# A five-layer graph network on one core: the first layer reads a transposed copy, the first and the fifth use a split ring

## The reference

```python
def _sage_conv(x, src, dst, Wl, bl, Wr):
    msg_sum = segment_sum(x[src], dst, num_segments=N_NODES)
    deg = segment_sum(ones_like(src), dst, num_segments=N_NODES)
    mean = msg_sum / maximum(deg, 1.0)[:, None]
    return mean @ Wl.T + bl + x @ Wr.T

x = layernorm(x + conv_a2(relu(conv_a1(x))))
x = layernorm(x + conv_b3(relu(conv_b2(relu(conv_b1(x))))))
```

## Time and profile before

| | us |
|---|---|
| median of 3 runs | 5494.6 (5491.9 to 5495.12) |
| the profiled execution | 5473.94 |
| its span, first to last instruction | 5472.3 |
| PE busy | 5178.4 |
| DVE busy | 3574.3 |
| ACT busy | 2560.0 |
| POOL busy | 2278.1 |
| groups of a1 and the end of its pass, window | 159.5 to 922 |
| groups of a2, window | 948 to 1821 |
| b1 and b2 | 1821 to about 4258 |
| groups of b3, window | 4292 to 5462 |

### The profile page before, as it was taken

How to read it: one execution, slowest core, us unless ns; L and a number is a source line. 1 busy time by engine, 2 the same in 40 slices (tenths; PEclk the granted TensorE clock), 3 DMA queues, 4 the chain that set the end, 5 groups by cost and what they waited for, 6 DMA issues and landing times. The chain is left out here.

```text
span 5472.3 us, 161658 instructions
## 1 busy us (share of the span) xinstructions
PE 5178.4 (95%) x44358; PEld 5110.7 (93%) x44359; DVE 3574.3 (65%) x9610; ACT 2560.0 (47%) x7254; POOL 2278.1 (42%) x2959
## 2 busy tenths in 40 slices
PE   1999998999999899999989999999999899999999
PEld 0899998889888899999989999999999899999999
DVE  4344444777777788888866666666666455555555
ACT  0343433777777433333333333333333466666666
POOL 1665655555555344444432322322222333333332
PEclk9999999999999999999999999999999999999999
DMA  1555554666667566666655555555555566666666
GB/s 29 150 168 164 172 167 143 202 202 206 205 200 208 164 194 192 194 195 195 193 165 177 173 178 176 174 179 174 174 180 169 178 217 219 217 219 220 216 219 195
DMA packets 1322822, 1006.82 MB, mean 184 GB/s; under 512 B 70406, under 2 KB 1278627, under 8 KB 1322756
## 3 DMA queue, kind: packets, MB, share of 16 engines
q1 hardware_dynamic: 1247044, 825.23, 48.6%
q0 software_dynamic: 75712, 180.76, 10.7%
HBM read 645.58 MB, written 360.13 MB: 184 GB/s over the span
## 5 line engine op out<-in xcount | busy, mean ns | idle before, releaser
L1043 PE MATMUL f_product_b<-f_ring_b,f_onehot_b 128*128 x6272 | 996.5, 281 | 0.0
L690 PE MATMUL m_product_a<-m_ring_a,m_onehot_a 128*128 x6272 | 959.8, 276 | 0.0
L1043 PEld LDWEIGHTS f_product_b<-f_ring_b,f_onehot_b 128*128 128x128 f32 x6272 | 855.8, 188 | 0.0
L1099 ACT ACTIVATE f_ring_b<-f_e_product_b,t_rec_all 128x256 f32 (+1 forms) x784 | 328.9, 471 | 1099.1 <-PE f_e_product_b L1056 1091.1
L792 DVE TENSOR_TENSOR m_onehot_a<-iota_all,t_win_all 128x512 f32<-128x512 f32 x784 | 537.5, 686 | 454.4 <-PE m_product_a L690 388.4
L690 PEld LDWEIGHTS m_product_a<-m_ring_a,m_onehot_a 128*128 128x128 f32 x6272 | 829.5, 193 | 0.0
L1037 PE MATMUL f_product_b<-b_r_all,f_t_hi_b 128*128 128x256 f32 x2352 | 723.2, 307 | 0.0
L1039 PE MATMUL f_product_b<-b_r_all,f_t_lo_b 128*128 128x256 f32 x2352 | 661.0, 281 | 0.0
L1038 PE MATMUL f_product_b<-b_r_all,f_t_hi_b 128*128 128x256 f32 x2352 | 659.4, 280 | 0.0
L686 PE MATMUL m_product_a<-a_r_all,m_t_full_a 128*128 128x128 f32 x3136 | 608.0, 276 | 0.0
L976 POOL TENSOR_TENSOR f_held_b<-ones_all 1x1 f32<-1x1 f32 x390 | 71.4, 183 | 1236.0 <-ACT f_e_idx_b L1081 1157.1
(11 more groups left out here) (193 smaller groups left out, 12135.2 us busy)
## 6 DMA issues: line engine op xcount, KB each, us to landing
g<-f_rows_out_b SPq DMA_DIRECT2D x392, 512.0 KB
f_rows_in_b<-g SPq DMA_DIRECT2D x196, 512.0 KB
m_rows_in_b<-g SPq DMA_DIRECT2D x196, 512.0 KB
m_rows_in_a<-in_x_dram SPq DMA_DIRECT2D x196, 256.0 KB
h<-m_rows_out_a SPq DMA_DIRECT2D x196, 256.0 KB
m_rows_in_a<-h SPq DMA_DIRECT2D x196, 256.0 KB
m_res_in_a<-in_x_dram SPq DMA_DIRECT2D x196, 256.0 KB
x<-m_rows_out_a SPq DMA_DIRECT2D x196, 256.0 KB
```

Source lines behind the costliest of these rows:

```text
L690: mm = pe.matmul(to, onehot[:, s, n, :], ring[:, bass.ds(at[n] * fo, fo)], start=False, stop=(w == 1), skip_group_check=True)
L1043: mm = pe.matmul(to, onehot[:, s, n, :], ring[:, bass.ds(at[n] * (2 * fo) + half * fo, fo)], start=False, stop=(w == 1 and half == 1))
```

## The change

`steps` is replaced, in narrow passes only, by `phased`, which unrolls six groups an iteration and hands each step an object `At` in place of numbers. It keeps each engine's order but for what follows.

- a1 gets `flat=x_flat`, a copy of the input that the host transposed, 128 rows of 100000. SP loads 128 x 512 pieces of it straight into `t_full`, which gets three buffers; `turn_nodes` and `nodes_full` fall away, and each load waits for the product that last read its buffer.
- a1 and b3 get `split=True`. A ring slot holds 256 columns of type fp32r: a high part that ScalarE writes as before, and a low part, the rest of the value, that VectorE writes (`ring_low`). `onehot` is fp32r too. One matmul of 256 columns adds both parts into a product of two banks. The bias is added by two matmuls with 256 columns. ScalarE copies the low halves of the product to SBUF (`low_part`, new tile `part`), and VectorE adds high and low. `low_part(g-1)` is the first instruction of ScalarE's step, and waits for the product g-1.
- b3: VectorE's add no longer has the residual. GpSimd adds it (`mix`) behind its gathers, and `moments` waits for that. SP's load of the residual waits for the mix.

`cv.get("ahead", 2)` stays 2 for all layers, so the gathers keep two slots. The diff, cut to the core:

```diff
+def phased(pr, eng, step):
+    ...
+    with eng.Fori(1, turns) as turn:
+        for m in range(PHASES):
+            step(At(m, turn), At(m + LEAD, turn))
...
+    flat, split = cv.get("flat"), cv.get("split", False)
+    D = cv.get("ahead", 2)
+    R = 3 if flat is not None else 2
+    C = 2 if split else 1
...
+        t_full = pr.sb(c, "m_t_full", [P, R, kt, GROUP])
+        onehot = pr.sb(c, "m_onehot", [P, 2, 2 * T, P], F32R if split else F32)
+        ring = pr.sb(c, "m_ring", [P, RING * C * fo], F32R if split else F32)
+        product = [pr.ps(c, f"m_product{i}", (P, C * 512)) for i in range(2)]
...
+            def load_rows(g):
+                if flat is not None:
+                    wait(sp, s_product, g.n(1 - R))
+                    sp.dma_start(t_full[:, g.slot(R), 0, :], flat[:, bass.ds(base(g), GROUP)]
+                                 ).then_inc(rows_here[g.slot(R)].sem, 16)
...
+            def load_res(g):
+                wait(sp, s_total, g.n(-1))
...
+            def mix(g):
+                s = g.slot(2)
+                wait(pool, res_here[s], g.turn(2) + 1)
+                wait(pool, s_sum, g.n(1))
+                pool.tensor_tensor(total[:, s, :, :], total[:, s, :, :], res_in[:, s, :, :],
+                                   ALU.add).then_inc(s_mixed.sem, 1)
+            def step(g, p):
+                if p is not None and (p.reg is not None or p.off + D < G):
+                    wait(pool, s_index, p.n(D + 1))
+                    wait(pool, s_held, p.n(1))
+                    mark().then_inc(s_held.sem, 1)
+                    gather(p.plus(D))
+                if norm and split and has(g, 1):
+                    mix(g.plus(-1))
...
+                if split:
+                    pe.matmul(halves(s)[:, 2 * u:2 * u + 2, 0, :], pr.two_rows[:, :], cv["bias_row"][:, 0:2, :],
+                              start=True, stop=False, skip_group_check=True)
...
-                        mm = pe.matmul(to, onehot[:, s, n, :], ring[:, bass.ds(at[n] * fo, fo)], start=False,
-                                       stop=(w == 1), skip_group_check=True)
+                        mm = pe.matmul(both, onehot[:, s, n, :], ring[:, bass.ds(at[n] * (C * fo), C * fo)],
+                                       start=False, stop=(w == 1), skip_group_check=True)
...
+            def low_part(g):
+                s = g.slot(2)
+                wait(act, s_product, g.n(1))
+                wait(act, s_sum, g.n(-1))
+                act.activation(part[:, s, :, :], halves(s)[:, :, 1, :], ACT.Copy).then_inc(s_part.sem, 1)
...
+            def step(g, p):
+                if split and has(g, 1):
+                    low_part(g.plus(-1))
+                if p is not None:
+                    edges_full(p)
+                    if p.reg is not None or p.off + D < G:
+                        take_numbers(p.plus(D))
...
+            def ring_low(p):
+                wait(v, s_ringhi, p.n(1))
+                for a in range(2):
+                    at = ((p.n(0, 2) + a) % RING) * (C * fo)
+                    ins = v.scalar_tensor_tensor(out=ring[:, bass.ds(at + fo, fo)], ...
+                ins.then_inc(s_ring.sem, 1)
+            def moments(g):
+                s = g.slot(2)
+                wait(v, s_total, g.n(1))
```

More of the change, by code:

```diff
@@ L19 @@
 LEAD = 6
+PHASES = 6
 BEHIND, AHEAD = 12, 5
@@ L513, in steps, with __init__, n, slot @@
         step(g, None, g % 2, g // 2, None)
+class At:
+    def __init__(self, off, reg=None):
+        self.off, self.reg = off, reg
+    def n(self, more=0, times=1):
+        at = (self.off + more) * times
+        return at if self.reg is None else self.reg * (PHASES * times) + at
+    def slot(self, depth):
+        return self.off % depth
+    def turn(self, depth):
+        at = self.off // depth
+        return at if self.reg is None else self.reg * (PHASES // depth) + at
+    def plus(self, k):
+        return At(self.off + k, self.reg)
+    def below(self, k):
+        return self.reg is None and self.off < k
+def phased(pr, eng, step):
+    G = pr.groups
+    for p in range(LEAD):
+        step(None, At(p))
+    turns = (G - LEAD) // PHASES
+    for g in range(PHASES):
+        step(At(g), At(g + LEAD))
+    with eng.Fori(1, turns) as turn:
+        for m in range(PHASES):
+            step(At(m, turn), At(m + LEAD, turn))
+    for g in range(turns * PHASES, G - LEAD):
+        step(At(g), At(g + LEAD))
+    for g in range(G - LEAD, G):
+        step(At(g), None)
+def uses(G, depth):
+    return [len(range(n, G, depth)) for n in range(depth)]
 def narrow_pass(pr, cv):
@@ L596, in _ @@
-            load_rows(2, 0)
-            def step(g, s, more):
-                if not (isinstance(g, int) and g >= G - 3):
-                    load_rows(g + 3, 1 - s)
-                if has(g, late):
-                    store(g - late, (s - late) % 2)
-                if more and norm:
-                    load_res(g + 2, s)
-            for g in (0, 1):
-                step(g, g, True)
-            with sp.Fori(1, G // 2 - 2) as i:
-                for s in range(2):
-                    step(i * 2 + s, s, True)
@@ new lines, in step @@
+            def step(g, p):
+                if g is None:
+                    if p.off < ahead:
+                        load_rows(p)
+                        if norm and p.off < 2:
+                            load_res(p)
+                    return
+                if g.reg is not None or g.off + ahead < G:
+                    load_rows(g.plus(ahead))
+                if has(g, late):
+                    store(g.plus(-late))
+                if norm and (g.reg is not None or g.off + 2 < G):
+                    load_res(g.plus(2))
@@ L781, in _, with compare @@
-            steps(pr, act, step)
+            for p in range(D):
+                take_numbers(At(p))
+            phased(pr, act, step)
+            if split:
+                low_part(At(G - 1))
             if norm:
-                normalise(G - 2, 0, G // 2 - 1)
-                deviation(G - 1, 1)
-                normalise(G - 1, 1, G // 2 - 1)
+                normalise(At(G - 2))
+                deviation(At(G - 1))
+                normalise(At(G - 1))
         @block.vector
         def _(v):
-            def compare(g, s, u):
-                wait(v, s_product, g - 1)
+            def compare(g, u):
+                s = g.slot(2)
+                wait(v, s_product, g.n(-1))
```

348 lines of the change are left out of this document (192 added, 156 removed).

## The result

The changed kernel takes **5743.0 us** (median of 4 runs, 5741.4 to 5754.42) against 5494.86 us before (median of 4, 5491.9 to 5500.39): 1.0457 times as long, 95% interval 1.0442 to 1.0472. The forecast was 5699 us in a range of 5600 to 5860. The profiled execution took 5754.42 us.

What follows compares the result with a forecast made beforehand. TensorE was taken to bound b3 and a1 before, closed chains through GpSimd, VectorE and ScalarE (b3) and through the gathers (a1) after. 5473.9 + 208 (b3) + 3 (its end) - 6 (a1) + 20.7 = 5699 us, range 5600 to 5860.

Steps and rivals of the forecast that it cites:

- Rival 1: TensorE stays the bound in b3 and a1, which get faster: 5181 us; chance 0.06.
- the three waits: b3, once a group: GpSimd's mark for take_numbers, VectorE's moments for the mix, ScalarE's deviation for the moments; cycle 7.07 us.
- the mix: b3: GpSimd's 128x512 residual add, without a row in the trace, taken at 1.14 us, between 0.68 and 1.92.
- The other links: b3: the closed one-group chain without the mix, from low_part through gathers and moments to deviation, 5.93 us.
- Rival 2: b3: the mix is slow, 1.92 us, by inputs in turn or VectorE's traffic; 7.85 a group, 5851 us; chance 0.10.
- The chain of two groups: a1: a loop through product, low_part, gathers, landing and transposes, 7.48 us for two groups, 3.74 a group.
- landing: a1: from the second gather's end until the transposes start, 1.60 us, with 0.3 left below and 0.8 above.
- the 0.14 that I had carried over: a1: us a group the old stage needed beyond its slots, added to 3.74 to give 3.88.
- Rival 3: a1: TensorE's completions seen late, now on the chain, 0.8 us a group, +159 us, 5858 us; chance 0.08.
- Rival 5: TensorE, now waiting, is granted less clock; at half in all of a1, +316 us, 6015 us; chance 0.05.
- Rival 6: b3: the ring stays two instructions of 256 columns, TensorE at 6.1 us, no time lost; no separate chance given.
- Rival 4: a1: the landing overlaps and the stage falls to GpSimd's pace, 3.12 us a group, 5551 us; chance 0.05.

Runs made afterwards that it cites:

- run 3: Changed kernel with one more 128x512 GpSimd add, of the residual with itself into a spare buffer, ahead of each mix in b3: 5959.2 us.
- run 4: Changed kernel with b3's residual added by VectorE ahead of its moments instead of by GpSimd: 5520.2 us.
- run 9: Changed kernel with four unread identity transposes a group added on TensorE in a1, ahead of the gathered rows' transposes: 5758.7 us.
- Runs 7 and 8: Changed kernel with, first, a third buffer for a1's gathers: 5652.4 us; second, low_part behind take_numbers in a1 instead: 5651.9 us.
- run 5: Changed kernel with the mix ahead of the mark and the two gathers in GpSimd's step: 5671.5 us.
- run 11: Changed kernel with three gather buffers and low_part behind take_numbers in a1 and b3, and the mix at the head of GpSimd's step: 5320.0 us.

## Why the prediction was right, and where it was off

**The bound and its loss.** TensorE lost the work that was forecast and stopped being the bound in both stages, as the prediction said. Rival 1 (TensorE still the bound) fell with the waits of b3.

**b3, +208 forecast, +222 measured.** The mechanism is shown: the three waits stand where they were named, a doubled add lengthens the group one for one (run 3), and taking the mix out of the chain removes the loss (run 4). The group was forecast at 7.07 us and took 7.11. Inside the sum the mix was mis-sized, 1.14 where 1.28 us were measured. The changed kernel's rows of it (shortest, median, longest ns):

```profile
L701 POOL TENSOR_TENSOR m_total_b<-m_total_b,m_res_in_b x196: 1259/1284/1592, 4355.1 to 5740.5; 128x512 f32<-128x512 f32 x196
```

The other links came to 5.83 in place of 5.93. Four times GpSimd's iota plus a start was a fair estimate for an add that has no row, and low by 0.14 us, 27 us in all. The Trainium skill (GPSIMD Engine Reference, sections 3.1 and 4.1) gave 1.12 by a quarter of its figure; the trace is 0.16 above it. The old stage was 5.97 by the same measure as 7.11, not 6.00, the other few microseconds. Rival 2 (1.92 us) did not come: nothing competed with the mix, as was argued: beside 189 of the 196 VectorE made no one-hot, and each of these took under 1.4 us. TensorE was busy 78% in b3's window (1081.11 of 1388.10), forecast 72 to 75. The sum of slots was right: the weight loads, whose rows lie end to end, are busy 1010.32 us, 73% and 5.18 us a group. The matmuls' rows are drawn longer than a slot (two wide ones 0.48 us, where their two loads take 0.23), and each pause adds such a tail.

**a1, -6 forecast, +60 measured.** The chain of two groups was right and one of its terms was not. The same links in the changed kernel, against the earlier trace rows (the transposes at 443.75 and two groups on at 451.91):

```profile
443.75 0.43 PE L730 MATMUL m_e_turned_a<-ident_all,m_e_rows_a 128*128 128x128 f32 x2 [1.56 <-DMA m_e_rows_a<-in_x_dram,m_e_idx_a]
...
445.34 0.60 ACT L842 ACTIVATE m_part_a<-m_product_a 128x512 f32<-128x512 f32 x1 [2.27 <-PE m_product_a L777]
...
446.10 0.21 ACT L813 ACTIVATE m_e_idx_a<-t_src_all 128x2 int32 x1
...
446.47 0.18 POOL L687 TENSOR_TENSOR m_held_a<-ones_all 1x1 f32<-1x1 f32 x1 [1.89 <-ACT m_e_idx_a L813]
...
448.53 0.99 POOL L692 DMA_INDIRECT m_e_rows_a<-in_x_dram,m_e_idx_a  x1 [0.30 <-issue]
...
451.91 0.43 PE L730 MATMUL m_e_turned_a<-ident_all,m_e_rows_a 128*128 128x128 f32 x2 [1.84 <-DMA m_e_rows_a<-in_x_dram,m_e_idx_a]
```

| link | forecast | here |
|---|---|---|
| transposes and second half of the product, seen by ScalarE | 1.58 | 1.59 |
| low_part and e_full, to take_numbers | 0.80 | 0.76 |
| take_numbers to the mark | 0.38 | 0.37 |
| mark to the second gather's end | 3.12 | 3.05 |
| landing | 1.60 | 2.39 |
| sum | 7.48 | 8.16 |

The term that failed is the landing. Over a1, in the 86 groups where TensorE stood idle over 0.4 us for its gathered rows, they came 2.38 us (median) after the second gather's end. I read 1.60 off one place of the old trace, where TensorE did not wait; such a row says only what a landing can be, and it was about the shortest one, for no transposes of a1, in the old kernel or the changed one, started sooner than 1.6 us after their gather. The old trace had better places: the six where TensorE did wait have 2.4 to 3.6 us, median 2.9. As far as six places tell, the landing did not grow with the change, it was misread. My reason for taking it, that TensorE waited only 5.1 us for gathers, spoke of cover, not of length. The bound I gave above it, 0.8, was just wide enough. The pair of groups is 0.68 longer than forecast, 0.34 a group; the 0.14 that I had carried over from a stage bound by TensorE does not come on top; the mean group (4.20) is 0.12 over the pair shown. 0.34 - 0.14 + 0.12 = 0.32, times 195 is 62 of the 66 us by which a1 was missed; the old stage, 3.89 and not 3.91 by this measure, is the rest. The Trainium skill (DMA: Bandwidth & Descriptors, on the anatomy of one DMA from GpSimd) puts the fixed cost of such a transfer at about 2.0 us, most of it until the end is confirmed; the trace has 2.38 from the end of the issue, and the 2.0 would have been the better term.

Rival 3 (a1 loses through late completions) had the right sign and the wrong agent: it is the transfer that is late, each time, not TensorE's end now and then. Rival 5 (the clock) is refuted as the main cause by run 9, although the clock did fall; a cost of some 10 us is not excluded. Runs 7 and 8 show the chain: either of the two ways of opening it gives 92 to 118 us in the stage. That a1 moved by less than 80 us, and that bn_stats waits for GpSimd, are the two points on which the prediction staked itself; both held.

**a2, nothing forecast, -13 measured.** Every kernel here with the new loop has a2 at 4.37 to 4.41 us a group, the one before 4.47. Its instructions are the same; the loop body is now six groups long. That the longer body is the reason was not tested. **Rival 6** (the ring's matmul as two instructions) did not occur: L777 shows 4704 matmuls over a1 and a2 together, 8 a group in a1 and 16 in a2's plain ring, and b3's window has 8894 TensorE instructions for 10311 before. **Rival 4** (a1 at GpSimd's pace, 3.12) was reached by no run; the best is 3.56.

**The sum.** 5474 + 222 + 60 - 13 + 5 + 3, and a few in the gaps, against the profiled 5754. Part of the closeness of 5699 to 5743 is luck. The forecast grows the time by 205 us; the medians grew by 248, and the two profiled executions, from which the stages are read, by 279, so the stages' terms miss by 74 us and not by 43. Two errors in b3 had opposite signs (the mix 0.14 us longer, the other links 0.10 shorter), and a2's 13 us, which the forecast did not have, hid a part of a1's miss.

## What to carry over

When a change frees the bounding engine, do not price what it frees; walk each engine's queue for loops that close over one group or over the depth of a buffer, and sum the links. Then do the same for the loop that your cure would make: run 5 moved an add and only swapped a one-group chain for a two-group one, and it took a third buffer to collect the gain. The add on the slow engine cost 1.1 us a group behind the gathers. At the head of the step, with three buffers and low_part behind the take (run 11), VectorE waited for it 8.6 us in all, although each add was longer: its place decided, not its length.

A transfer's landing is read only where somebody waits for it. A row in which nobody waits bounds it from above for that one time, and the luckiest of them is no mean.

When long groups and a half clock stand together, fill the pause with idle work before blaming the clock, and look at the links at either clock, as the filler has a price of its own.

## What was not expected of the hardware

- GpSimd's 128x512 add took 1284 ns while VectorE waited for it, and 1642 ns (median; 1262 to 1654) where it ran beside VectorE's one-hot and ring work (run 11), 28% more. In run 11 the only two adds under 1.4 us were the two beside which VectorE did neither. The Trainium skill (GPSIMD Engine Reference, section 8) names such sharing with VectorE instructions that have two SBUF inputs, and the trace agrees. With one operand read for both inputs it took 1054 ns mean (run 3).

```profile
L701 POOL TENSOR_TENSOR m_total_b<-m_total_b,m_res_in_b x196: 1262/1642/1654, 4212.1 to 5298.0; 128x512 f32<-128x512 f32 x196
```

- A gather's landing grew with the stage: 2.38 us in a1 with rows of 128 floats, 4.6 us (median of 123 waited for) in run 5's b3 with rows of 256 floats and more traffic beside it (193 GB/s in b3 against 154 in a1). Which of the two makes it longer was not tried.
- The granted clock fell to 0.50 (1.2 GHz) in stretches of a1 that came, nearly all, within some 2 us after a pause of TensorE of 1.4 to 2.5 us (28 stretches); 24 other pauses of 1.5 to 2.7 us passed without a fall. Four idle transposes a group took most of the stretches away and no time with them.
